# One of two copies of the transposed probabilities, taken from ScalarE to VectorE in a decoder's cross attention

## The chip, the cores and the metric

The kernel runs on one core of a Trainium2 chip. The metric is the device time of one execution in microseconds (us). For the kernel before, three executions gave 2287.59, 2289.07 and 2291.86 us; the median is 2289.07. The engines are written as in the profile: PE is TensorE (PEld its weight loads), ACT ScalarE, DVE VectorE, POOL GpSimd, and SP the engine that only starts transfers.

## What is computed

The reference is one decoder layer with three parts, each added to its input: a gated delta-rule attention, cross attention to a context, and a feed-forward part with block-quantised weights and activations. The change touches only the second:

```python
qh = q.reshape(b, s, N_GROUPS, HEADS_PER_GROUP, HEAD_DIM).transpose(0, 2, 3, 1, 4)
kh = k.reshape(b, s, N_GROUPS, HEAD_DIM).transpose(0, 2, 1, 3)
vh = v.reshape(b, s, N_GROUPS, HEAD_DIM).transpose(0, 2, 1, 3)
scores = jnp.einsum('bghsd,bgtd->bghst', qh, kh) * scale
probs = jax.nn.softmax(scores, axis=-1)
out = jnp.einsum('bghst,bgtd->bghsd', probs, vh)
...
return out @ Wc.T + bc
```

There are 8 batches of 256 tokens, 4 groups of 4 heads with 32 channels each, and 256 context rows (used as keys and as values). All is float32.

## The kernel before

Three functions follow one another. `attend` is the second: it projects the first attention's output (W_out, three matmuls for each product, since operands are split in a high and a low part), does the cross attention, and, beside that, quantises the feed-forward weights on VectorE and GpSimd. It runs from about 1560 to 2040 us of the profile. Each engine has its own instruction list, written out by hand; waits are on semaphores, and an engine works strictly in the order of its list.

**The tiles.** A batch has eight tiles (c, u): group c = 0 to 3, and u = 0 or 1 for the half of 128 tokens. I call the time between two tiles' scores a slot and name it by the tile whose scores open it. The lists run through the slots (0,0), (0,1), (1,0) to (3,1); `last_tile(b, c, u)` is the tile one slot earlier. Batches are called 0 to 7 here; batches 0 and 1 and the last two are written out, the others are a loop.

**One slot on each engine.**

- PE: `scores` of this tile (line 1531; it waits for `pt0_done` and `pt1_done` of the tile two slots before, which had the same `ps_s` banks), `turn_probs` of the last tile (line 1539, eight transposes into `ps_s[u][0]` and `ps_s[u][1]`), one to three pieces of `project` for the next batches (lines 1493 to 1495, six matmuls a piece; slots (0,1) and (1,0) have one piece each), and `mix` of the last tile (line 1549), whose first half (k = 0) waits for `pt0_done` and second half (k = 1) for `pt1_done`. In slots (3,1) and (0,0) `spread` (line 1560) comes ahead of `mix`; it waits for `rs_done`, VectorE's reciprocals. In (0,0) `keys(b, 1)` (line 1517) ends the slot, in (0,1) and (1,0) `combine(b - 1, u)` (lines 1573 to 1575).
- ACT: `turned` of the last tile (lines 1687 to 1692), the two copies from `ps_s` to `probs_t`; then `weigh` of this tile (line 1682), four exponentials that wait for VectorE's maxima. In (3,1) and (0,0) `spread` (line 1698) stands between the two.
- DVE: in some slots first `finish` (1830) and `residual` (1785), then `maxima` of this tile (line 1805, two instructions), `reciprocals` (1812) in (3,1) and (0,0), `weighted` (1819) in (0,0) and (0,1), `mixed` (1823) of the batch before in (0,1) and (1,0), then `split` (1777), layer norm (1798) and the steps of a weight chunk (1885 to 1914).
- POOL: the chunk's elementwise steps (2034 to 2050) and the powers.

`mix` for c = 0 writes `ps_v[u]` anew, so it also waits for the `mixed` of the batch before: `pe.wait_ge(mlo_done[u], b)`. For u = 0 that happens in slot (0,1), for u = 1 in (1,0). After batch 6 there are no more projections, so in batch 7, and in slots (3,0) and (3,1) of batch 6, there is nothing of `project` between `turn_probs` and `mix`.

Of the kernel before, what the change touches and what calls it, by code (L numbers as in the profile page):

```python
# [12 lines left out]
ACT = mybir.ActivationFunctionType  # L13
# [3 lines left out]
B, T, D = 8, 256, 512  # L17
# [1203 lines left out]
def attend(nc, ident, neg_half, x, ctx_in, out_t, W_out, Wc, bc, w_gate, w_up, w_down, x2_dram, xq_dram, wq_dram):  # L1221
# [10 lines left out]
    HEADS, GROUPS, HD = 16, 4, 32  # L1232
# [11 lines left out]
    with ExitStack() as st:  # L1244
        def sb(name, shape, dt):
            return st.enter_context(nc.sbuf_tensor(name, shape, dt))
# [4 lines left out]
        def two(name):  # L1251
            return [sem(f"{name}{u}") for u in U]
# [29 lines left out]
        probs_t = [sb(f"probs_t{u}", [P, 2, PER, P], F32) for u in U]  # L1282
# [24 lines left out]
        ps_s = [[st.enter_context(nc.psum_tensor(f"ps_s{u}{i}", [P, 2 * T], F32)) for i in range(2)] for u in U]  # L1307
# [17 lines left out]
        pt_ps, pt0_done, pt1_done, pv_ps = two("pt_ps"), two("pt0_done"), two("pt1_done"), two("pv_ps")  # L1325
# [12 lines left out]
        def last_tile(b, c, u):  # L1338

            return (b, c, 0) if u else (b, c - 1, 1) if c else (b - 1, GROUPS - 1, 1)  # L1340
# [3 lines left out]
        with nc.Block() as block:  # L1344
# [299 lines left out]
            def _(act):  # L1644
# [42 lines left out]
                def turned(b, c, u):  # L1687
                    act.wait_ge(pt_ps[u], GROUPS * b + c + 1)
                    act.wait_ge(pv_ps[u], GROUPS * b + c)
                    for k, done in enumerate((pt0_done, pt1_done)):  # L1690
                        act.activation(probs_t[u][:, k, :, :].rearrange("p j s -> p (j s)"), ps_s[u][k][:, :],  # L1691
                                       ACT.Copy).then_inc(done[u], 1)

                def spread(b, u):

# [70 lines left out]
                step(B - 2, True, True, False)  # L1766
                step(B - 1, True, False, False)
                turned(B - 1, GROUPS - 1, 1)
                spread(B - 1, 1)
                for u in U:  # L1770
# [3 lines left out]
            def _(dve):  # L1774
                def split(b, u, e):
                    dve.wait_ge(o_hi_done[e], 2 * b + u + 1)
                    dve.tensor_tensor(o_lo[e][:, :, :], o_raw[e][:, :, :], o_hi[e][:, :, :].bitcast(F32),
                                      ALU.subtract).then_inc(o_lo_done[e], 1)

                def residual(b, u):  # L1780

                    dve.wait_ge(y_ps[u], b + 1)
                    dve.wait_ge(x_dma[u], 16 * (b + 1))
                    dve.wait_ge(x1b_done[u], b)
                    dve.tensor_tensor(x1[u][:, :], x_in[u][:, :], ps_y[:, :], ALU.add).then_inc(x1_done[u], 1)

                def variance(b, u):
                    dve.wait_ge(x1_done[u], b + 1)
                    dve.bn_stats(stats[u][:, :], x1[u][:, :])
                    dve.drain()  # L1790
                    dve.bn_aggr(moments[u][:, :], stats[u][:, :]).then_inc(stat[u], 1)
                    dve.wait_ge(stat[u], b + 1)
                    dve.tensor_scalar(var_eps[u][:, :], moments[u][:, 1:2], LN_EPS, None, ALU.add).then_inc(var_done[u], 1)

                def layernorm(b, u):
                    dve.wait_ge(rstd_done[u], b + 1)
                    dve.wait_ge(t_ps[u], b)
                    dve.tensor_scalar(xn[u][:, :], x1[u][:, :], moments[u][:, 0:1], rstd[u][:, 0:1], ALU.subtract,
                                      ALU.mult).then_inc(xn_done[u], 1)

                def maxima(b, c, u):
                    dve.wait_ge(s_ps[u], GROUPS * b + c + 1)
                    dve.wait_ge(exp_done[u], GROUPS * b + c)
                    for i in range(2):
                        last = dve.tensor_reduce(neg_max[u][:, 2 * i:2 * i + 2],  # L1805
                                                 ps_s[u][i][:, :].rearrange("p (j t) -> p j t", j=2), AX_X, ALU.max, negate=True)
                    last.then_inc(max_done[u], 1)

                def reciprocals(b, u):
                    dve.wait_ge(exp_done[u], GROUPS * (b + 1))  # L1810
                    dve.wait_ge(spread_ps[u], b)
                    dve.reciprocal(r_sums[u][:, :], sums[u][:, :]).then_inc(rs_done[u], 1)

                def weighted(b, u):

                    dve.wait_ge(pv_ps[u], GROUPS * (b + 1))
                    dve.wait_ge(spread_done[u], b + 1)
                    mixed_heads = ps_v[u][:, :, :].rearrange("p k t -> p (k t)")
                    dve.tensor_tensor(mixed_heads, mixed_heads, r_chan[u], ALU.mult).then_inc(weighted_done[u], 1)

                def mixed(b, u):
                    dve.wait_ge(mhi_done[u], b + 1)
                    dve.tensor_tensor(mix_lo[u][:, :, :], ps_v[u][:, :, :], mix_hi[u][:, :, :].bitcast(F32),
                                      ALU.subtract).then_inc(mlo_done[u], 1)

                def finish(b, u):
                    dve.wait_ge(c_ps[u], b + 1)
                    dve.wait_ge(x1b_done[u], b + 1)
                    dve.wait_ge(x2_dma[u], 16 * b)
                    dve.tensor_tensor(x2[u][:, :], ps_t[:, :], x1b[u][:, :], ALU.add).then_inc(x2_done[u], 1)  # L1830

                def token_variance(b, u):

                    dve.wait_ge(x2_done[u], b + 1)
                    dve.bn_stats(q_stats[u][:, :], x2[u][:, :])
                    dve.drain()
                    dve.bn_aggr(q_moments[u][:, :], q_stats[u][:, :])
                    dve.drain()
                    dve.tensor_scalar(q_var[u][:, :], q_moments[u][:, 1:2], LN_EPS, None, ALU.add).then_inc(q_var_done[u], 1)
# [76 lines left out]
                def step(b, before, after, further):  # L1916
                    for c in range(GROUPS):
                        for u in U:
                            if before and (c, u) in ((1, 0), (1, 1)):
                                finish(b - 1, u)  # L1920
                            if after and (c, u) in ((1, 1), (3, 0)):
                                residual(b + 1, 1 - u)
                            maxima(b, c, u)
                            if before and (c, u) == (0, 0):
                                reciprocals(b - 1, 1)
                            if (c, u) == (GROUPS - 1, 1):
                                reciprocals(b, 0)
                            if before and c == 0:
                                weighted(b - 1, u)
                            if before and (c, u) in ((0, 1), (1, 0)):  # L1930
                                mixed(b - 1, c)
                            if after and (c, u) in ((1, 0), (1, 1)):
                                split(b + 1, 1, u)
                            if after and (c, u) == (3, 1):
                                layernorm(b + 1, 1)
                            if further and (c, u) in ((2, 1), (3, 1)):
                                split(b + 2, 0, c - 2)
                            if after and (c, u) in ((1, 1), (3, 0)):
                                variance(b + 1, 1 - u)
                            if (c, u) not in ((1, 1), (2, 1)):  # L1940
                                chunk(b, (0, 1, 2, None, 3, None, 4, 5)[2 * c + u])
                            if after and (c, u) == (2, 0):
                                layernorm(b + 1, 0)
                            if before:
                                if (c, u) == (1, 1):
                                    for tile in U:
                                        token_variance(b - 1, tile)
                                if (c, u) == (2, 0):
                                    token_norms(b - 1)
                                if (c, u) == (2, 1):  # L1950
                                    token_scales(b - 1)
                                if (c, u) == (3, 0):
                                    token_rounds(b - 1)
# [28 lines left out]
                    step(b, True, True, True)  # L1982
                step(B - 2, True, True, False)
                step(B - 1, True, False, False)
                reciprocals(B - 1, 1)
                for u in U:
                    weighted(B - 1, u)
# [479 lines left out]
```

## Time and profile before

| | us |
|---|---|
| median of three executions | 2289.07 |
| the profiled execution's own time | 2291.95 |
| span of the profiled execution, first to last instruction | 2290.2 |
| mean granted TensorE clock (share of full speed) | 0.948 |

The profile is of one execution. In the rows below, "busy" is time inside instructions, and a wait in square brackets is the idle time in front of an instruction with the one that released it. A row of several instructions (x8) shows the start of the first and the time to the end of the last. Consecutive instructions of an engine overlap a little, so the distance of two starts is what one costs in a full queue.

### The profile page before, as it was taken

Reading aid. Unit: us, or ns where it says so; the run is one execution under the profiler, and the core shown is the slowest. Engines: PE = TensorE matmul, PEld = TensorE weight load, DVE = VectorE, ACT = ScalarE, POOL = GpSimd, SP = SyncE. Lnnn points to the kernel's source line nnn. Section 1 sums busy time; section 2 is a strip of 40 time slices with the busy share of each in tenths; the row PEclk is TensorE's granted clock in tenths of the full one; section 3 lists DMA queues with packets and bytes.
Section 4 is the critical chain, followed back from the end, with each engine's and each line's share of the span. In section 5 each row is a group of like instructions: output and inputs, shape, how many; then the busy total and the mean of one; then the engine's idle time right before and its main releaser. Section 6 shows DMA issues by size and latency. Waiting matters only on the chain. (4 is left out here: it accounts for less than half of the span.)

```text
span 2290.2 us, 56662 instructions
## 1 busy us (share of the span) xinstructions
PE 2065.7 (90%) x19672; PEld 1502.0 (66%) x19672; DVE 1732.6 (76%) x4021; ACT 1530.1 (67%) x4330; POOL 709.5 (31%) x610
## 2 busy tenths in 40 slices
PE   5599899899899899899899899858999999857998
PEld 3477677677677677677677677646666666534544
DVE  7677777778777777777777777745788888755997
ACT  3588788788788788788778778735666656533343
POOL 6312112112111211211211211213576666751332
PEclk8799999999999999999999999859999999978999
DMA  3100100100100100100100100043333333222111
GB/s 76 52 10 18 38 10 12 44 10 9 47 10 9 47 10 9 47 10 9 36 21 9 33 24 9 33 143 102 99 100 101 101 101 104 67 95 81 56 53 48
DMA packets 122930, 108.19 MB, mean 47 GB/s; under 512 B 12080, under 2 KB 97072, under 8 KB 122800
## 3 DMA queue, kind: packets, MB, share of 16 engines
q1 hardware_dynamic: 122800, 106.87, 14.9%
q14 instruction: 99, 0.81, 0.1%
q8 instruction: 31, 0.51, 0.1%
HBM read 72.24 MB, written 34.60 MB: 47 GB/s over the span
## 5 line engine op out<-in xcount | busy, mean ns | idle before, releaser
L588 PE MATMUL proj<-xn_hi,w_lo 128*128 x768 | 367.5, 478 | 0.0
L589 PE MATMUL proj<-xn_lo,w_hi 128*128 x768 | 308.2, 401 | 0.0
L590 PE MATMUL proj<-xn_hi,w_hi 128*128 x768 | 306.9, 400 | 0.0
L973 DVE SCALAR_TENSOR_TENSOR qkv<-conv_in,taps,qkv 128x512 f32<-128x512 f32 x384 | 279.4, 748 | 0.0
L1194 POOL TENSOR_TENSOR o_scale<-o_var,neg_half 128x4 f32<-128x4 f32 x68 | 67.6, 1010 | 572.8 <-DVE o_var L994 572.7
L1210 POOL TENSOR_TENSOR k_len<-sumsq,pos_half 128x4 f32<-128x4 f32 x32 | 47.1, 1472 | 601.5 <-DVE sumsq L1141 601.5
L1085 DVE TENSOR_TENSOR i_less_r<-bank_c,join_mask 128x256 f16<-128x256 f32 x330 | 124.6, 418 | 104.1 <-PE bank_c L652 103.5
L892 ACT ACTIVATE inv<-bank_b 128x256 f16<-128x256 f32 x330 | 112.3, 382 | 120.2 <-PE bank_b L673 116.3
L590 PEld LDWEIGHTS proj<-xn_hi,w_hi 128*128 128x128 f32 x768 | 146.8, 191 | 35.2
L588 PEld LDWEIGHTS proj<-xn_hi,w_lo 128*128 128x128 f32 x768 | 146.4, 191 | 24.3
L1691 ACT ACTIVATE probs_t<-ps_s 128x512 f32<-128x512 f32 x128 | 69.5, 596 | 134.1 <-PE ps_s L1539 134.1
L839 ACT ACTIVATE g_mask<-mask_ge,g_cols 128x128 fp32r<-128x128 f32 x528 | 158.1, 408 | 0.0
L589 PEld LDWEIGHTS proj<-xn_lo,w_hi 128*128 128x128 f32 x768 | 148.2, 193 | 8.3
L1493 PE MATMUL ps_y<-wo_hi,o_lo 128*128 128x512 f32 x256 | 108.9, 426 | 21.8 <-DVE wo_lo L1959 18.4
L673 PEld LDWEIGHTS bank_b<-i_less_r,inv_t 64*64 64x64 f16 x2640 | 72.7, 111 | 83.3 <-issue 83.3
L673 PE MATMUL bank_b<-i_less_r,inv_t 64*64 64x64 f16 x2640 | 99.9, 198 | 27.1 <-DVE i_less_r L1085 23.5
L1805 DVE TENSOR_REDUCE neg_max<-ps_s 128x2 f32<-128x512 f32 x128 | 82.0, 682 | 54.1 <-PE ps_s L1531 53.3
L1682 ACT ACTIVATE probs<-ps_s,neg_max 128x256 f32<-128x256 f32 x256 | 117.9, 485 | 5.1 <-DVE neg_max L1805 5.1
L1114 DVE TENSOR_TENSOR v_r<-v,bank_b 128x256 fp32r<-128x256 f32 x132 | 55.6, 421 | 83.1 <-PE bank_b L700 81.4
L2308 ACT ACTIVATE g_silu<-ps_g 128x512 f32<-128x512 f32 x64 | 38.2, 597 | 118.8 <-PE ps_u L2247 118.8
L2417 POOL TENSOR_TENSOR i_q<-i,i_scale 128x1024 bf16<-128x1024 fp8e4 x32 | 61.1, 1909 | 167.5 <-DVE i L2374 167.5
L1495 PE MATMUL ps_y<-wo_hi,o_hi 128*128 128x512 f32 x256 | 102.6, 401 | 0.0
(288 smaller groups left out, 5830.4 us busy)
## 6 DMA issues: line engine op xcount, KB each, us to landing
out_t<-o_out SPq DMA_DIRECT2D x68, 256.0 KB, 2.0
o_raw<-out_t SPq DMA_DIRECT2D x32, 512.0 KB, 5.6
w_raw<-in_L_attn_W_qkv_dram SPq DMA_DIRECT2D x36, 256.0 KB, 2.9
wq_dram<-wq_q SPq DMA_DIRECT2D x48, 128.0 KB, 2.3
w_raw<-in_L_attn_W_z_dram SPq DMA_DIRECT2D x18, 256.0 KB, 2.7
x_sb<-in_x_dram SPq DMA_DIRECT2D x16, 256.0 KB, 2.8
x_in<-in_x_dram SPq DMA_DIRECT2D x16, 256.0 KB, 5.8
wq_raw<-in_L_ffn_w_gate_dram SPq DMA_DIRECT2D x16, 256.0 KB, 2.8
```

What stands on the lines that cost most here:

```text
L588: pe.matmul(out, w_lo[:, k, cols], sh.xn_hi[:, k, tok], start=(k == 0), stop=False)
L589: pe.matmul(out, w_hi[:, k, cols], sh.xn_lo[:, k, tok], start=False, stop=False)
L590: product = pe.matmul(out, w_hi[:, k, cols], sh.xn_hi[:, k, tok], start=False, stop=(k == KT - 1))
L673: last = pe.matmul(folded(bank_b[s])[rows, hb, :], inv_t[s][rows, hb, :], i_less_r[s][rows, hb, :], start=True, stop=True)
L839: last = act.activation(g_mask[s][:, i, hb, :], sh.mask_ge[:, :], ACT.Copy, scale=g_cols[:, s, 4 * i + hb:4 * i + hb + 1])
L892: act.activation(inv[s][:, :, :], folded(bank_b[s]), ACT.Copy).then_inc(t_done[s], 1)
L973: dve.scalar_tensor_tensor(out=out, in0=conv_in[:, j, :, k:k + T], scalar=taps[:, j, k:k + 1], in1=out, op0=ALU.mult, op1=ALU.add).then_in ...
L1085: dve.tensor_tensor(i_less_r[s][:, :, :], folded(bank_c[s]), bcast(sh.join_mask[:, l + 1, :], 1, 4), ALU.mult).then_inc(r_done[s], 1)
L1493: pe.matmul(ps_y[:, :], o_lo[e][:, g, :], wo_hi[:, k, :], start=begin, stop=False)
L1495: product = pe.matmul(ps_y[:, :], o_hi[e][:, g, :], wo_hi[:, k, :], start=False, stop=end)
L1682: last = act.activation(probs[u][:, j, :], ps_s[u][j // 2][:, T * (j % 2):T * (j % 2) + T], ACT.Exp, bias=neg_max[u][:, j:j + 1], accum_ou ...
L1805: last = dve.tensor_reduce(neg_max[u][:, 2 * i:2 * i + 2], ps_s[u][i][:, :].rearrange("p (j t) -> p j t", j=2), AX_X, ALU.max, negate=True)
```

## The change

ScalarE's `turned` keeps the copy for k = 0 and loses that for k = 1. VectorE gets a `turned` of its own with the copy for k = 1, with the same two waits. In every slot it stands right behind `maxima`, and so ahead of `reciprocals`, `weighted` and `mixed`; the last tile's copy stands ahead of the closing `reciprocals`. The semaphores `pt0_done` and `pt1_done` and who waits for them are as before.

```diff
@@ scalar
                 def turned(b, c, u):
                     act.wait_ge(pt_ps[u], GROUPS * b + c + 1)
                     act.wait_ge(pv_ps[u], GROUPS * b + c)
-                    for k, done in enumerate((pt0_done, pt1_done)):
-                        act.activation(probs_t[u][:, k, :, :].rearrange("p j s -> p (j s)"), ps_s[u][k][:, :],
-                                       ACT.Copy).then_inc(done[u], 1)
+                    act.activation(probs_t[u][:, 0, :, :].rearrange("p j s -> p (j s)"), ps_s[u][0][:, :],
+                                   ACT.Copy).then_inc(pt0_done[u], 1)
@@ vector
+                def turned(b, c, u):
+                    dve.wait_ge(pt_ps[u], GROUPS * b + c + 1)
+                    dve.wait_ge(pv_ps[u], GROUPS * b + c)
+                    dve.tensor_copy(probs_t[u][:, 1, :, :].rearrange("p j s -> p (j s)"),
+                                    ps_s[u][1][:, :]).then_inc(pt1_done[u], 1)
...
                             maxima(b, c, u)
+                            if before or c + u:
+                                turned(*last_tile(b, c, u))
                             if before and (c, u) == (0, 0):
                                 reciprocals(b - 1, 1)
...
                 step(B - 1, True, False, False)
+                turned(B - 1, GROUPS - 1, 1)
                 reciprocals(B - 1, 1)
```

## Rows read from the trace of the kernel before

**Rows 1.** The page's first part: busy time, share of the span, instructions

```profile
PE 2065.7 (90%) x19672; PEld 1502.0 (66%) x19672; DVE 1732.6 (76%) x4021; ACT 1530.1 (67%) x4330; POOL 709.5 (31%) x610
```

**Rows 2.** Busy time by stretch: batch 1, batch 5, and the end of batch 7

```profile
core 0: us, PE busy (x) PEld busy (x) DVE busy (x) ACT busy (x) POOL busy (x), PEclk, DMA share, GB/s
1628.30:1685.10 56.80, 53.66 (x424) 37.25 (x425) 46.69 (x97) 35.76 (x101) 40.06 (x34) 1.00 0.36 103
...
1860.00:1919.50 59.50, 56.53 (x426) 39.14 (x426) 48.23 (x99) 35.76 (x101) 40.06 (x36) 0.94 0.34 101
...
2001.60:2020.40 18.80, 13.04 (x120) 6.67 (x120) 18.24 (x44) 12.70 (x42) 16.50 (x16) 1.00 0.20 65
```

**Rows 3.** Waits of PE, batches 1 to 6: us in total, times, longest

```profile
PE ps_c L1517 <- ACT q_t L1663: 15.5, 6, 2.6
...
PE ps_s L1560 <- DVE r_sums L1812: 2.0, 1, 2.0
...
PE ps_v L1549 <- DVE mix_lo L1823: 0.4, 2, 0.3
```

**Rows 4.** Longest wait of ACT other than for the transposes, batches 1 to 6

```profile
ACT r_chan L1698 <- PE ps_s L1560: 28.6, 12, 2.7
```

**Rows 5.** Timeline of PE, batch 1, slot (0,1): start us, us, engine, line

```profile
1637.92 0.66 PE L1517 MATMUL ps_c<-ident,k_rep 128*128 128x128 f32 x4 [2.59 <-ACT q_t L1663]
...
1642.22 0.65 PE L1549 MATMUL ps_v<-probs_t,ctx_v 128*32 128x128 f32 x16 [0.18 <-DVE mix_lo L1823]
```

**Rows 6.** Timeline of DVE: batch 1, slots (0,1) and (1,0); batch 5, slot (0,1)

```profile
1640.89 0.69 DVE L1819 TENSOR_TENSOR ps_v<-ps_v,r_chan 128x512 f32<-128x512 f32 x1
1641.48 0.68 DVE L1823 TENSOR_TENSOR mix_lo<-ps_v,mix_hi 128x512 fp32r<-128x512 f32 x1
...
1648.17 0.68 DVE L1823 TENSOR_TENSOR mix_lo<-ps_v,mix_hi 128x512 fp32r<-128x512 f32 x1
...
1874.57 0.68 DVE L1823 TENSOR_TENSOR mix_lo<-ps_v,mix_hi 128x512 fp32r<-128x512 f32 x1
```

**Rows 7.** Timeline of ACT, batch 1, slot (0,1)

```profile
1641.02 1.08 ACT L1691 ACTIVATE probs_t<-ps_s 128x512 f32<-128x512 f32 x2
```

**Rows 8.** Timeline of PE, batch 1, end of slot (1,0)

```profile
1648.94 0.40 PE L1495 MATMUL ps_y<-wo_hi,o_hi 128*128 128x512 f32 x1
1649.27 0.32 PE L1549 MATMUL ps_v<-probs_t,ctx_v 128*32 128x128 f32 x4
```

**Rows 9.** Groups by line over the whole span: busy, mean ns of one, idle before

```profile
L1691 ACT ACTIVATE probs_t<-ps_s 128x512 f32<-128x512 f32 x128 | 69.5, 596 | 134.1 <-PE ps_s L1539 134.1
...
L1910 DVE TENSOR_SCALAR wq_step<-wq_step 128x512 f32<-128x512 f32 x48 | 20.4, 426 | 0.0
...
L1819 DVE TENSOR_TENSOR ps_v<-ps_v,r_chan 128x512 f32<-128x512 f32 x16 | 10.9, 681 | 0.0
```

**Rows 10.** Timeline of PE, batch 5, slot (0,1)

```profile
1872.65 1.97 PE L1539 MATMUL ps_s<-ident,probs 128*128 128x128 f32 x8
...
1876.60 0.65 PE L1549 MATMUL ps_v<-probs_t,ctx_v 128*32 128x128 f32 x16
```

**Rows 11.** Timeline of DVE: batch 2 (2,0), batch 3 (3,1), batch 4 (0,0)

```profile
1722.26 0.46 DVE L1798 TENSOR_SCALAR xn<-x,moments,rstd 128x512 f32<-128x512 f32 x1
...
1797.38 1.33 DVE L1798 TENSOR_SCALAR xn<-x,moments,rstd 128x512 f32<-128x512 f32 x1
...
1805.10 0.24 DVE L1812 RECIPROCAL r_sums<-sums 128x16 f32<-128x16 f32 x1
```

**Rows 12.** Timeline of PE, batch 4, slot (0,0)

```profile
1807.08 1.08 PE L1560 MATMUL ps_s<-ident,r_sums 128*32 128x128 f32 x32
```

**Rows 13.** Timeline of PE, batch 7: slots (0,0), (2,0) and (3,1)

```profile
1979.87 1.08 PE L1560 MATMUL ps_s<-ident,r_sums 128*32 128x128 f32 x32 [1.86 <-DVE r_sums L1812]
...
2007.39 0.92 PE L1549 MATMUL ps_v<-probs_t,ctx_v 128*32 128x128 f32 x16 [0.69 <-ACT probs_t L1691]
...
2020.48 1.08 PE L1560 MATMUL ps_s<-ident,r_sums 128*32 128x128 f32 x32 [1.51 <-DVE r_sums L1812]
```

## The prediction

> **What bounds the kernel now.** I read the busy shares first, then busy time by batch inside `attend`, then PE's waits, then the timelines of PE, DVE and ACT side by side, slot by slot. Over the whole span PE leads with 90%, DVE follows with 76%, ACT has 67% [rows 1]. The change lies in `attend` alone, so shares of the whole say little. In a full batch PE is busy 53.66 of 56.8 us, DVE 46.69, ACT 35.76 [rows 2]. So ACT, the engine that is relieved, has the most room of the three, and the one that is loaded has less.
>
> PE's list sets the pace in batches 1 to 6. It stands idle for one thing only in every batch: `keys(b, 1)` waits 2.59 us for ACT's `q_t` [rows 5], six times, 15.5 us in all [rows 3]. Before the `q_t` copy ACT does `turned`, `spread` and the exponentials, so a shorter `turned` looks useful there. It isn't: `spread` on ACT must first wait for PE's own `spread`, and that stands behind two pieces of `project` in PE's list. ACT's waits for it, in (3,1) and (0,0), are twelve with 28.6 us, 2.4 us each [rows 4]. The copy is taken from a stretch that ends in a wait.
>
> Batch 7 is another regime. With no `project` in it, PE waits for both: for ACT's copies (0.69 us ahead of `mix`) and for VectorE's reciprocals (1.86 and 1.51 us ahead of `spread`) [rows 13]. From 2001.6 to 2020.4 DVE is busy 18.24 of 18.8 us, ACT only 12.70 [rows 2]. DVE is the bound there, with half a microsecond to spare.
>
> **The price of the copy.** ACT loses 64 copies of 596 ns (half of the 128 in [rows 9]); in a full queue each frees 0.49 us (two take 1.08 [rows 7]). DVE gains 64. No float32 copy from PSUM by DVE is in the trace. The bounds are the one-input DVE instruction of the same size between SBUF tiles, 426 ns, and a two-input one that reads PSUM, 681 ns [rows 9]. I take 0.68 us, the row that shares type, size and source memory, and 0.60 us for what it adds to a full queue (the distance of the starts at 1640.89 and 1641.48 [rows 6]). The low end is 0.34 us a copy in the queue. The Trainium skill has a rule for this (VectorE: DVE Perf Modes, "Why PSUM operands drop a tier"): a PSUM operand excludes the mode that doubles a float32 copy's rate. No copy in this trace tests it; by it the upper price holds, and with the mode the low end of the sum would.
>
> **Slot (0,1), batches 1 to 6.** `mix` of tile (0,0) needs `mixed` of the batch before, which VectorE now reaches one copy later. In batch 1 `mix_lo` ends at 1641.48 + 0.68 = 1642.16, ACT's second copy at 1642.10 [rows 6, 7], and `mix` starts at 1642.22, 0.06 us behind the later, having waited [rows 5]. One copy ahead of it moves `mix` by the full 0.60. The same three rows come again in batches 2 to 4 (`mix` 0.25 us behind `mix_lo`'s end), where I take the same, so 4 x 0.60 = 2.4 us. In batches 5 and 6 PE itself ran slow here, the transposes taking 1.97 us [rows 10], so that `mix`, at 1876.60, came 1.35 us after `mix_lo` had ended [rows 6, 10]. There VectorE has also to wait for those late transposes before it can copy, and `weighted` and `mixed` queue behind; I make it 0.1 us each, 0.2 in all.
>
> **Slot (1,0), batches 1 to 6.** `mix_lo` ends at 1648.85 [rows 6], and `mix` starts at 1649.27 at its own pace, 0.33 us behind the last projection [rows 8]. Room: 0.42 - 0.06 = 0.36 us. The copy takes that up and 0.24 us more: 6 x 0.24 = 1.4 us. PE gets none of this back later, for its next wait, that for `q_t`, hangs on PE's own `spread` and moves with it. Batch 0 has no `mixed`; there only a `residual` that PE waits for can come later, between 0 and 0.6 us, of which I take 0.2, since VectorE sits in waits for GpSimd in front of it.
>
> **Other slots of batches 1 to 6: nothing.** The tightest is `spread` in (0,0). The reciprocals end at 1805.34 [rows 11] and PE takes them up at 1807.08 [rows 12]: 1.7 us of room. Ahead of them come the copies of (0,0), of (3,1) and of (3,0). The one of (3,1) fits into a stretch in which the layer norm instruction took 1.33 us where it needs 0.46 elsewhere, held by GpSimd [rows 11]. That leaves about 1.1 us. If this cover fails, 1.7 us stand against 1.7, so the cost would still be near nothing. The `mix` of these slots comes 2 us or more after the transposes, behind `project`, so an earlier second copy brings it nothing.
>
> **The seam, batch 6 slot (3,1) to batch 7 slot (0,0).** Both `spread`s wait for the reciprocals already (2.0 us [rows 3], 1.86 us [rows 13]) and VectorE never idles in between. Three copies come in, one is covered as above: 1.2 us.
>
> **Batch 7.** (0,1): 0.6 for the copy and 0.2 because it waits for slow transposes, 0.8. (1,0): here `mix` had no room, 0.6. From (1,1) to the reciprocals of (3,1), five copies are 3.0 us on a VectorE with some 0.5 us of idle time [rows 2]; ACT's 0.49 us a slot is of no use once the maxima are what the exponentials wait for. Of the rest a bit is lost in holds by GpSimd that are there anyway: 2.4 us. The closing copy ahead of the last reciprocals: 0.1.
>
> **The sum.** 2.4 + 0.2 + 1.4 + 0.2 (batch 0) + 1.2 + 0.8 + 0.6 + 2.4 + 0.1 = 9.3 us longer. The profiled execution took 2291.95 us, 0.13% above the median; against it this is 2301.2, against the median of 2289.07 it is 2298.4, which I forecast. At 0.34 us a copy, (0,1) costs 4 x 0.34, (1,0) nothing, the seam 0.7, batch 7 about 0.6 + 0.3 + 1.0: some 4 us, 2293. With no cover anywhere (0.6 in batch 0, 0.6 in (0,1) of batches 5 and 6, 1.8 at the seam, 3.0 at the end) it is 12.1, so 2301.
>
> **Rivals.** A measurement of this kernel tells some 0.2% (4.6 us) from no change.
>
> *ACT's relief decides at the end (faster).* In slots (1,1) to (3,1) of batch 7 and (3,0) of batch 6 PE waits 0.69 us for the copies [rows 13] and the exponentials begin only behind both. If VectorE's copy is cheap enough that each slot's maxima are still done when ACT's single copy is, every such slot saves 0.49 us: six make 2.9 us. It decides if a copy adds less than about 0.36 us, since then (1,0) costs nothing as well and (0,1) only about 1.4 us. Net 1.5 us less, 2287.5, and 2286 if (0,1) were hidden too. Against it stands VectorE's 97% in that stretch. To come out faster by over 0.2% more than this mechanism has would be needed; a share of chance goes there for what I can't see.
>
> *Absorbed (same).* VectorE loses up to 1 us at a time to GpSimd (1.33 against 0.46 us [rows 11]). If the copies, reading PSUM, pass while GpSimd holds the port, the later steps wait less, and the seam and the end cost under 1 us each. Then (0,1), (1,0) and a little more remain, 4 us: 2293.
>
> *TensorE's clock (slower still).* The granted clock was 1.00 in batch 1, which took 56.8 us, and 0.94 in batch 5, which took 59.5, with the same work [rows 2]; the slow stretch follows the 2.59 us wait in (0,0), and 0.94 means a few us at the lower level, 1.2 GHz. Batches 2 to 4 lie between. If the moved waits bring batch 1 into it and lengthen two others, 1.4 + 2 x 1.2 = 3.8 us come on top: 2302. The other way it could give back 2 us.
>
> *Held by GpSimd (slower still).* The layer norm instruction takes up to 0.87 us more than elsewhere when GpSimd is at work [rows 11]. Were the copy held like that, it would add that much in (0,1) and (1,0) of six batches, 10.4 us, and 2304 or later at the end. Against it: the DVE instructions that read PSUM keep to 0.68 us on average [rows 9]. The Trainium skill (SBUF — State Buffer, "Who interferes with whom") has copies in a two-port mode fight GpSimd for a port, which would be this rival if the mode held with a source in PSUM.
>
> **Chances.** The forecast with its bounds, 2294 to 2303: 0.62. Absorbed: 0.16. ACT's relief: 0.11, of which 0.06 is beyond 0.2%. Clock or port beyond 2303: 0.11. The band of 0.2% ends at 2293.6: faster 0.06, same 0.19, slower 0.75. The range leaves out the faster end and the port: 2290 to 2305.
>
> **What the changed profile would show.** A DVE COPY `probs_t` of about 0.68 us, 64 times. In (0,1) and (1,0) PE's `mix` waits for `mix_lo`, twelve times instead of two. The distance between batches' first scores grows by 0.8 us in batches 1 to 4 and less in 5 and 6. In batch 7, `spread` waits over 3 us for `r_sums`, the exponentials wait for `neg_max`, and DVE shows no idle time from (1,1) to (3,1). I am wrong if the copy takes under 0.45 us, if `mix` starts as early as before, or if the batch 7 slots get shorter.

## The result, and the profile after

The change makes the kernel slower by 0.43%: the ratio of the times is 1.0043, with a 95% interval of 1.0033 to 1.0052. The medians of 20 executions each are 2298.49 us after (2291.27 to 2304.43) and 2288.31 us before (2285.28 to 2295.39). The profiled execution after took 2301.67 us, with a span of 2299.9, so both profiled executions lie 3 to 4 us above their medians.

The page's busy shares after answer to [rows 1]:

```profile
PE 2066.6 (90%) x19672; PEld 1501.3 (65%) x19672; DVE 1764.0 (77%) x4085; ACT 1501.2 (65%) x4266; POOL 699.8 (30%) x610
```

ACT lost 29 us of work, DVE gained 31, and the time grew. The groups by line give the price of the copy, beside [rows 9]; the mean of one is in ns behind the busy us:

```profile
L1823 DVE COPY probs_t<-ps_s 128x512 f32<-128x512 f32 x64 | 43.5, 680 | 4.6 <-PE ps_s L1539 4.6
...
L1690 ACT ACTIVATE probs_t<-ps_s 128x512 f32<-128x512 f32 x64 | 38.3, 599 | 158.2 <-PE ps_s L1539 158.1
```

The 680 ns are those of the row with a PSUM operand, 681 ns. The idle time ahead of ACT's copies grew from 134.1 to 158.2 us: most of what ScalarE saved, it now waits.

Busy time after in batch 1, batch 2 and batch 5, beside [rows 2]; the granted clock stands behind POOL's busy time:

```profile
1627.70:1685.30 57.60, 53.69 (x424) 37.21 (x425) 50.13 (x106) 32.02 (x93) 37.51 (x33) 1.00 0.35 102
1685.30:1745.30 60.00, 56.73 (x426) 39.24 (x426) 52.05 (x107) 32.22 (x93) 39.17 (x35) 0.94 0.33 101
...
1863.60:1921.40 57.80, 53.68 (x424) 37.22 (x425) 51.90 (x107) 32.06 (x93) 39.18 (x35) 1.00 0.35 104
```

Batch 1 has 0.8 us more at the same clock of 1.00 and the same PE work (53.69 against 53.66 us). Batch 5 is shorter than before, at 1.00 instead of 0.94, and batch 2 longer, at 0.94 where it had 0.97.

So in batch 1 the slots can be laid side by side. PE and then DVE in the slots (0,1) and (1,0) after, beside [rows 5, 6, 8]:

```profile
1637.32 0.66 PE L1517 MATMUL ps_c<-ident,k_rep 128*128 128x128 f32 x4 [2.59 <-ACT q_t L1663]
1637.90 1.13 PE L1531 MATMUL ps_s<-k_blocks,q_t 64*128 64x512 f32 x4
...
1642.21 0.64 PE L1549 MATMUL ps_v<-probs_t,ctx_v 128*32 128x128 f32 x16 [0.78 <-DVE mix_lo L1828]
...
1645.78 1.13 PE L1531 MATMUL ps_s<-k_blocks,q_t 64*128 64x512 f32 x4
...
1649.50 0.65 PE L1549 MATMUL ps_v<-probs_t,ctx_v 128*32 128x128 f32 x16 [0.17 <-DVE mix_lo L1828]
```

```profile
1639.08 1.29 DVE L1804 TENSOR_REDUCE neg_max<-ps_s 128x2 f32<-128x512 f32 x2 [4.05 <-PE ps_s L1531]
1640.28 0.68 DVE L1823 COPY probs_t<-ps_s 128x512 f32<-128x512 f32 x1
1640.88 0.69 DVE L1818 TENSOR_TENSOR ps_v<-ps_v,r_chan 128x512 f32<-128x512 f32 x1
1641.48 0.68 DVE L1828 TENSOR_TENSOR mix_lo<-ps_v,mix_hi 128x512 fp32r<-128x512 f32 x1
...
1646.96 1.29 DVE L1804 TENSOR_REDUCE neg_max<-ps_s 128x2 f32<-128x512 f32 x2 [0.38 <-PE ps_s L1531]
1648.16 0.68 DVE L1823 COPY probs_t<-ps_s 128x512 f32<-128x512 f32 x1
1648.76 0.68 DVE L1828 TENSOR_TENSOR mix_lo<-ps_v,mix_hi 128x512 fp32r<-128x512 f32 x1
```

The copy stands between the maxima and what follows, one step of 0.60 us in the list. The wait of `mix` for `mix_lo` in (0,1) rises from 0.18 to 0.78 us, by exactly that step. In (1,0), where there was none, it is 0.17. The big wait for `q_t` is 2.59 us as before. PE's waits in batches 1 to 6, beside [rows 3]:

```profile
PE ps_c L1517 <- ACT q_t L1663: 15.6, 6, 2.6
PE ps_v L1549 <- DVE mix_lo L1828: 4.9, 11, 1.0
PE ps_s L1560 <- DVE r_sums L1811: 3.4, 1, 3.4
```

`mix` now waits eleven times where it had waited twice. The last row is the seam: `spread` in (3,1) of batch 6 waits 3.4 instead of 2.0 us.

At the end the waits of PE that have grown are those for VectorE. PE in batch 6 (3,1), then in batch 7 in (0,0), (0,1), (1,0), (2,1) and (3,1), beside [rows 13]:

```profile
1975.90 1.93 PE L1560 MATMUL ps_s<-ident,r_sums 128*32 128x128 f32 x32 [3.37 <-DVE r_sums L1811]
...
1983.39 1.08 PE L1560 MATMUL ps_s<-ident,r_sums 128*32 128x128 f32 x32 [0.94 <-DVE r_sums L1811]
...
1993.82 0.64 PE L1549 MATMUL ps_v<-probs_t,ctx_v 128*32 128x128 f32 x16 [1.98 <-DVE mix_lo L1828]
...
2002.65 0.65 PE L1549 MATMUL ps_v<-probs_t,ctx_v 128*32 128x128 f32 x16 [1.56 <-DVE mix_lo L1828]
...
2018.71 0.63 PE L1549 MATMUL ps_v<-probs_t,ctx_v 128*32 128x128 f32 x8 [1.74 <-DVE probs_t L1823]
...
2029.01 1.94 PE L1560 MATMUL ps_s<-ident,r_sums 128*32 128x128 f32 x32 [2.60 <-DVE r_sums L1811]
```

In two of the three `spread`s shown, the instructions themselves take 1.93 and 1.94 us in place of 1.08: behind the wait PE runs slow. That is no detail. The whole end, from the scores of (3,0) in batch 6 to `token_rounds` of batch 7, before and then after (granted clock behind POOL's busy time):

```profile
1964.91:2044.53 79.62, 53.29 (x496) 33.39 (x492) 60.28 (x136) 38.47 (x117) 55.41 (x50) 0.91 0.17 54
...
1966.31:2054.08 87.77, 58.17 (x496) 36.82 (x492) 65.12 (x148) 33.50 (x107) 55.95 (x52) 0.84 0.16 49
```

PE has the same 496 matmul instructions in both, and they take 4.9 us more at a granted clock of 0.84 instead of 0.91. Only the other 3.3 of the 8.15 us are added idle time of PE.

The table below serves the experiments too. "Batches 1 to 5" is the time from the first scores of batch 1 to those of batch 6. "End" is from the scores of (3,0) in batch 6 to the start of `token_rounds` of batch 7, the last part of `attend` that VectorE has. "PE busy" is the time inside PE's instructions in it, the same 496 in each kernel, and "clock" the granted clock there. Each is from one profile. e7 to e12 have `queries(b, 1)` earlier in ScalarE's list ("q early"), which is explained with e7.

| kernel | copy 2 made by | batches 1 to 5, us | end, us | PE busy in it, us | clock | ratio to before (95%) |
|---|---|---|---|---|---|---|
| before | ACT | 291.19 | 79.62 | 53.29 | 0.91 | 1 |
| changed | DVE | 293.71 | 87.77 | 58.17 | 0.84 | 1.0043 (1.0033 to 1.0052) |
| e1 | DVE at the end only | 290.24 | 87.37 | 57.76 | 0.82 | 1.0046 (1.0031 to 1.0062) |
| e2 | DVE, but for the end | 295.34 | 76.78 | 49.21 | 0.95 | 1.0015 (1.0004 to 1.0025) |
| e3 | DVE, but for (0,1), (1,0) | 292.23 | 85.94 | 58.12 | 0.83 | 1.0042 (1.0029 to 1.0055) |
| e4 | DVE, later in the slot | 290.36 | 81.66 | 53.95 | 0.88 | 1.0027 (1.0016 to 1.0038) |
| e5 | nobody | 292.20 | 76.40 | 49.80 | 0.94 | 1.0004 (0.9992 to 1.0016) |
| e6 | DVE, ACT kept busy | 293.59 | 86.20 | 55.69 | 0.87 | 1.0052 (1.0036 to 1.0068) |
| e7 | ACT, q early | 278.14 | 75.84 | 50.85 | 0.94 | 0.9925 (0.9909 to 0.9942) |
| e8 | DVE, q early | 278.45 | 83.98 | 56.16 | 0.84 | 0.9962 (0.9947 to 0.9977) |
| e9 | ACT, q early, reciprocals first | 278.17 | 77.26 | 51.43 | 0.92 | 0.9943 (0.9930 to 0.9957) |
| e10 | DVE later in the slot, else as e9 | 277.49 | 81.15 | 56.06 | 0.85 | 0.9935 (0.9922 to 0.9949) |
| e11 | as e7 | 278.14 | 75.15 | 49.24 | 0.95 | 0.9914 (0.9900 to 0.9929) |
| e12 | DVE later in the slot, q early | 277.87 | 80.48 | 53.62 | 0.87 | 0.9939 (0.9922 to 0.9956) |

With VectorE's copies in the end, the same matmuls take 53.62 to 58.17 us there, without them 49.21 to 53.29.

### The profile page after: what moved, and what is told of

Same layout as the page of the kernel before. It is cut to its first block and busy times, and to the rows that moved or that the text cites. A ratio compares the mean times of both kernels' runs of the same rounds, so it can differ in the third digit from the quotient of the medians.

```text
span 2299.9 us, 56726 instructions
## 1 busy us (share of the span) xinstructions
PE 2066.6 (90%) x19672; PEld 1501.3 (65%) x19672; DVE 1764.0 (77%) x4085; ACT 1501.2 (65%) x4266; POOL 699.8 (30%) x610
## 5 line engine op out<-in xcount | busy, mean ns | idle before, releaser
L1690 ACT ACTIVATE probs_t<-ps_s 128x512 f32<-128x512 f32 x64 | 38.3, 599 | 158.2 <-PE ps_s L1539 158.1
L1114 DVE TENSOR_TENSOR v_r<-v,bank_b 128x256 fp32r<-128x256 f32 x132 | 55.6, 421 | 83.7 <-PE bank_b L700 82.1
```

## The experiments

**Where the cost arises: e1 and e2.** Each kernel has the change in one stretch only. A predicate on the slot says who makes the second copy; both engines ask it (edits against the changed kernel, cut at the dots):

```diff
+        def on_vector(b, c, u):
+            return isinstance(b, int) and (b >= B - 1 or b == B - 2 and c == GROUPS - 1)
...
+                    for k, done in ((0, pt0_done), (1, pt1_done))[:2 if both else 1]:
+                        act.activation(probs_t[u][:, k, :, :].rearrange("p j s -> p (j s)"), ps_s[u][k][:, :],
+                                       ACT.Copy).then_inc(done[u], 1)
...
-                            if before or c + u:
+                            if (before or c + u) and on_vector(b, c, u):
                                 turned(*last_tile(b, c, u))
```

That is e1; e2 has `not (...)`. Expected of e1:

> VectorE has the second copy only from slot (3,0) of batch 6 on; before that ScalarE keeps both. My theory (VectorE is the bound there, ScalarE's relief is worth nothing): batches 0 to 5 as long as before, and 5 us more from (3,0) of batch 6 to the end of attend, so about 2293. Rival (ScalarE's copies are what PE waits for there, 0.69 us a slot): 3 us less, 2285. Rival (the loss comes from the clock or from batches 1 to 6): no change, 2288.

Expected of e2:

> The complement: VectorE has the second copy in batches 0 to 5 and in batch 6 up to (2,1), ScalarE keeps both from (3,0) of batch 6 on. My theory: about 0.8 us more in each of batches 1 to 4, some 0.3 in 5 and 6, 0.2 to 0.8 in batch 0, and the end as before: 4.5 to 5 us more, about 2293; the two halves add up to the whole change. Rival (only the end costs): 2288. Where a batch's granted clock differs its length differs by a microsecond or more on top.

e1: 2297.57 against 2288.27 us, ratio 1.0046. That is more than the 5 us expected; the sign is my theory's, the rival of a gain is out. Its batches 1 to 5 are as long as before, and its end is 87.37 us, 7.8 longer than the 79.62 of before. e2: 2292.93 us, ratio 1.0015, as expected. Its batches 1 to 5 took 295.34 us, 4.1 more. Its end runs the code of before and took 76.78, so a profile of the same code differs by 3 us there. Most of the loss is thus in the end, some 8 us or more, and 3 to 5 in the rest, where I had put about half in each. The medians of the two add up to 13.9 us, against the 10.2 of the change; the intervals are too wide to say whether the halves add up.

**Which slots of a full batch: e3.** The kernel of e1 with the predicate `(c, u) not in ((0, 1), (1, 0))` in all batches.

> VectorE has the second copy in six slots of every batch, but not in (0,1) and (1,0), where ScalarE keeps both. My theory (in batches 1 to 6 only mix_lo behind the copy in these two slots costs anything): batches 1 to 6 at the length of before at equal clock, PE's wait of mix for mix_lo back to about 0.4 us in sum; what is left is the seam and batch 7 from (1,1) on, 4 us: 2292. Rival (VectorE's added load costs PE in other slots, or the clock does): batches 1 to 4 stay 0.5 us or more longer, 2296 or later.

2299.36 us, ratio 1.0042 (1.0029 to 1.0055): not 2292. By its total alone this is the rival's 2296 or later. The mechanism holds nevertheless in the part that it was about. PE's waits in batches 1 to 6, where `mix_lo` is gone from the list:

```profile
PE ps_c L1520 <- ACT q_t L1666: 15.6, 6, 2.6
PE ps_s L1534 <- ACT r_chan L1701: 2.2, 6, 0.4
PE ps_v L1552 <- ACT probs_t L1694: 0.7, 1, 0.7
```

Batches 1 to 5 took 292.23 us, the same as in e5 (292.20), which has no DVE copy at all. So six copies a batch outside (0,1) and (1,0) cost PE nothing that can be seen beside the clock. In the end e3 pays 85.94 us, 6.3 more than before and 9.2 more than e2's, where 4 were expected. The end was mis-sized here too, and that accounts for 2 to 5 us of the 7 that were missed; where the others lie stays open.

**Load or place: e4.** VectorE's copy moves behind `reciprocals`, `weighted` and `mixed`:

```diff
                             maxima(b, c, u)
-                            if before or c + u:
-                                turned(*last_tile(b, c, u))
...
                             if before and (c, u) in ((0, 1), (1, 0)):
                                 mixed(b - 1, c)
+                            if before or c + u:
+                                turned(*last_tile(b, c, u))
```

> Same split of work, but VectorE's copy stands behind reciprocals, weighted and mixed in its slot instead of ahead of them. My theory (what costs is what queues behind the copy): the first half of mix no longer waits, the second half waits for the copy; eight matmuls of about 0.28 us cover part of it, so (0,1) costs 0.3 instead of 0.6 and (1,0) about nothing; at the seam one copy less is ahead of each spread, and one less ahead of the reciprocals of (3,1) in batch 7. Some 4.5 to 5.5 us more than before, 2293, half of the change's cost. Rival (the load counts, not the place): 2298 as with the change.

2294.53 us, ratio 1.0027 (1.0016 to 1.0038), near the 2293 expected: about 4 us of the 10 are the place, though this interval and the change's overlap a little. In batches 1 to 5 `mix` waits 1.5 us in all for `mix_lo`, where it waits 3.9 with the copy ahead. The end is 81.66 us, six shorter than with the copy ahead; 4.2 of these are PE's busy time. The first `spread` of the end shows both parts of that, a shorter wait and full speed after it:

```profile
1973.62 1.08 PE L1560 MATMUL ps_s<-ident,r_sums 128*32 128x128 f32 x32 [2.77 <-DVE r_sums L1811]
```

**What ScalarE's relief is worth: e5 and e6.** In e5 ScalarE makes the first copy, the second is left out, and PE waits for the first only (against the changed kernel; VectorE's two calls and the second wait of `scores` go too):

```diff
-                def turned(b, c, u):
-                    dve.wait_ge(pt_ps[u], GROUPS * b + c + 1)
...
-                        pe.wait_ge((pt0_done, pt1_done)[k][u], GROUPS * b + c + 1)
+                        if k == 0:
+                            pe.wait_ge(pt0_done[u], GROUPS * b + c + 1)
```

> ScalarE makes the first copy only and nobody the second; mix reads what lay in the second half of probs_t, and waits only for the first copy. Left out: the second copy of the turned probabilities, so half of the context rows are mixed with stale values. It shows what ScalarE's relief is worth alone. My theory: nothing in batches 1 to 6 (57 to 59 us each as before), since ScalarE waits for PE's spread anyway; at the end, from (3,0) of batch 6, 0.3 to 0.49 us in each of six slots and the closing one, 2 to 3 us less, 2286. Rival (ScalarE's copies hold PE in full batches too): 0.49 us or more a batch on top, 2283 or less.

2289.04 against 2288.63 us, ratio 1.0004 (0.9992 to 1.0016), where 2286 was expected. With a whole copy a slot dropped and nobody charged for it, no gain can be measured; the interval leaves room for 1.8 us. The slots of the end do get shorter in the trace, 3.60 us against 4.09 in (2,0) and (2,1) of batch 7, the 0.49 expected. That is 1 us for the two, and the next slot, (3,0), gives back 0.7 of it (4.81 us instead of 4.09). In full batches the `q_t` wait is 15.6 us, unchanged. In e6 the changed kernel gets a copy back on ScalarE that nobody needs:

```diff
                     act.activation(probs_t[u][:, 0, :, :].rearrange("p j s -> p (j s)"), ps_s[u][0][:, :],
                                    ACT.Copy).then_inc(pt0_done[u], 1)
+                    act.wait_ge(pt0_done[u], GROUPS * b + c + 1)
+                    act.activation(filler[:, :], probs_t[u][:, 0, :, :].rearrange("p j s -> p (j s)"), ACT.Copy)
```

> The change, and ScalarE gets a copy of equal size between SBUF tiles in place of the one that it lost, behind its own first copy; nobody waits for it. It shows VectorE's load without ScalarE's relief. My theory: the same as the change to 0.1%, 2298, at the most 1 us later, since the exponentials wait for VectorE's maxima or for PE's spread and not for ScalarE. Rival (ScalarE's relief had given back part of the cost): 3 us or more later than the change, 2301 to 2303.

2300.29 us, ratio 1.0052 (1.0036 to 1.0068) against the change's 1.0043 (1.0033 to 1.0052): not told apart. Batches 1 to 5 are 293.59 against 293.71 us. So e5 bounds the relief at 1.8 us. e6 agrees with none in full batches, but over the whole its interval does not rule out the 3 us of its rival.

**The wait that the change leaves alone: e7, e8, e11.** PE's 2.59 us ahead of `keys(b, 1)` are caused by ScalarE's list, in which `queries` stands behind the exponentials. ScalarE has 2.4 us of waiting for `spread` [rows 4] into which it fits:

```diff
                             if before and (c, u) == (0, 0):
+                                queries(b, 1)
                                 spread(b - 1, 1)
                             weigh(b, c, u)
-                            if before and (c, u) == (0, 0):
-                                queries(b, 1)
```

e7 is this in the kernel before, e8 in the changed one.

> The kernel before, with ScalarE's queries(b, 1) (the q_t copy of line 1663) taken from behind the exponentials of (0,0) to ahead of spread, where ScalarE waits over 2 us for PE's spread. If PE's wait of 2.59 us in keys(b, 1) is what ScalarE's list order costs, PE then waits only for the exponentials of (0,0) ahead of its transposes in (0,1), about 0.9 us later: 1.5 to 2 us less in each of seven batches and fewer slow stretches of the clock, 2273 to 2278. Rival (k_blocks or the exponentials take the wait's place): no change.

> The same move of queries(b, 1) in the changed kernel. With PE's big wait in (0,0) gone, the slots (0,1) and (1,0) start earlier against VectorE, whose copy stands ahead of mix_lo. My theory: the change costs at least as much on this base as on the old one, 10 to 14 us more than e7. Rival (the wait in (0,0) was what kept ScalarE's relief from showing): the change costs under 5 us on this base.

e7: 2270.33 against 2288.63 us, ratio 0.9925 (0.9909 to 0.9942), 18 us faster and 3 us better than the near end of what was expected. e11 is the same kernel again:

> The kernel of e7 once more, beside e12 on the same chip, to see how far a median of five or six runs repeats: 2268 to 2272. If it comes near e9's 2275.7, e9 and e7 are not told apart.

2268.75 against 2286.69 us, ratio 0.9914 (0.9900 to 0.9929). It beats both kernels of the case. PE around `keys` in e7, slots (0,0) and (0,1) of batch 1:

```profile
1633.06 0.62 PE L1549 MATMUL ps_v<-probs_t,ctx_v 128*32 128x128 f32 x16
1633.61 0.66 PE L1517 MATMUL ps_c<-ident,k_rep 128*128 128x128 f32 x4
1634.20 1.13 PE L1531 MATMUL ps_s<-k_blocks,q_t 64*128 64x512 f32 x4
1635.79 1.09 PE L1539 MATMUL ps_s<-ident,probs 128*128 128x128 f32 x8 [0.46 <-ACT probs L1682]
...
1639.22 0.82 PE L1549 MATMUL ps_v<-probs_t,ctx_v 128*32 128x128 f32 x16 [0.97 <-ACT probs_t L1691]
```

Smaller waits of 0.46 and 0.97 us take the place of the 2.59. All of batches 1 to 5 now last 55.6 us, where before they lasted 56.8 to 59.5. Busy time in two of them, with the granted clock in the column behind POOL's:

```profile
1628.30:1684.00 55.70, 53.88 (x425) 37.22 (x424) 46.44 (x97) 35.70 (x101) 39.51 (x34) 1.00 0.36 105
1684.00:1739.50 55.50, 53.68 (x425) 37.21 (x424) 48.73 (x98) 35.56 (x100) 40.55 (x34) 1.00 0.37 110
```

The clock is 1.00 in both, and the others have the same length: without the long wait there is no stretch at the lower level, 1.2 GHz. So of some 2.6 us a batch (291.19 - 278.14 = 13.05 us for five), 1.2 are waiting (56.82 of batch 1, which was at 1.00 before as well, less 55.6) and the others are the clock.

e8: 2279.80 us, ratio 0.9962 (0.9947 to 0.9977), 9.5 us behind e7, just under the 10 to 14 expected; the rival of under 5 is out. On this base the full batches of the change cost only 0.06 us each, 55.69 against 55.63. In (0,1) `mix` now waits for ScalarE's `probs_t`, so that VectorE's earlier second copy helps as much there as it hurts in (1,0). PE's waits in batches 1 to 6 of e8:

```profile
PE ps_v L1549 <- ACT probs_t L1690: 6.4, 7, 1.0
...
PE ps_v L1549 <- DVE mix_lo L1827: 1.0, 6, 0.2
```

The end is 83.98 us against 75.84 in e7 and 75.15 in e11, some 8 us, and nearly all of the difference. Most of it, 5.3 and 6.9 us, is PE's busy time.

**The end with the reciprocals first: e9 and e10.** In e9, e7's kernel with `reciprocals` ahead of `maxima`; in e10 VectorE's copy is in e4's place besides.

```diff
+                            if before and (c, u) == (0, 0):
+                                reciprocals(b - 1, 1)
+                            if (c, u) == (GROUPS - 1, 1):
+                                reciprocals(b, 0)
                             maxima(b, c, u)
```

> The kernel of e7 (both copies on ScalarE, queries(b, 1) ahead of spread), and VectorE's reciprocals taken from behind the maxima to ahead of them in (3,1) and (0,0). My theory (at the end PE's spread waits for whatever stands ahead of the reciprocals in VectorE's list): the spread waits of batch 6 (3,1), 2.0 us, and of batch 7 (3,1), 1.5 us, shrink by 1.2 us each, so some 2 us less than e7, 2268, and full batches as in e7. Rival (the reciprocals now wait for the exponentials of (3,1) and hold the maxima of (0,0) back): full batches 0.3 us or more longer, 2271 or later.

> The same with VectorE making the second copy, placed behind reciprocals, weighted and mixed. My theory: VectorE is the bound from batch 6 (3,0) on, so even the best place leaves 2 to 5 us against e9; full batches gain or lose under 0.2 us each. 2271. Rival (place was all of it): equal to e9 within 1 us, or earlier by the 0.49 us a slot that ScalarE is relieved of.

e9: 2275.72 against 2289.03 us, ratio 0.9943 (0.9930 to 0.9957), where 2268 was expected: no gain over e7, rather a loss, though the two ran on different chips. The mechanism is there, (3,1) of batch 6 took 4.82 us instead of 6.46, and full batches stay at 55.6. But (0,1) of batch 7 took 12.16 instead of 10.30 us, with this wait for `mix_lo` in it where e7 had 2.46 us:

```profile
1969.05 1.08 PE L1549 MATMUL ps_v<-probs_t,ctx_v 128*32 128x128 f32 x16 [3.61 <-DVE mix_lo L1822]
```

What was won at one VectorE wait was lost at the next: 1.15 us of the 1.86 are the longer wait. In e11, the code of e7, the same slot took 8.76 us behind the same wait of 2.46, so that the others are no more than two profiles of one kernel differ by. The median lies 5 us above e7's. The profiled execution, 2269.89 us, is the fastest of its five, and its `attend` is only 2 us longer than e7's, so where the rest of the 5 us lies stays open. e10: 2274.99 us, ratio 0.9935 (0.9922 to 0.9949), equal to e9 within the intervals. I had expected 2 to 5 us more than e9; its end has 3.9 more in the profiles (81.15 against 77.26 us), the median has nothing. So these two don't decide between load and place.

**Load or place once more: e12.** e7's list, the copy on VectorE in e4's place.

> queries(b, 1) early, reciprocals behind the maxima as in the kernel before, VectorE's copy behind reciprocals, weighted and mixed. On this base full batches have no long wait, so the place shows in them undisturbed. My theory: full batches of 55.5 us, 0.1 to 0.2 less than e7's 55.63 and e8's 55.69; from batch 6 (3,0) on some 4 us more than e7 against 8 with the copy ahead (e8). 2274. Rival (the load counts): 2279 as e8.

2275.38 against 2286.69 us, ratio 0.9939 (0.9922 to 0.9956), beside e11's 2268.75 on the same chip. Full batches are 55.47 to 55.77 us, level with e7. The end is 80.48 us, against 75.15 with both copies on ScalarE and 83.98 with the copy ahead. Both theories have their share: in this place VectorE's load still costs 5 us at the end, and the place ahead adds some 3.5. Of the 5 us, 4.4 are PE's busy time and 1.0 its idle time (53.62 against 49.24, 26.86 against 25.91), so the load costs more by the pace of PE than by its waits. Between e12 and e8 the ratios alone decide nothing (0.9939 against 0.9962, with intervals that overlap); the 3.5 us are those of the two profiles.

## Why the prediction was right, and where it was not

The sum was right: 9.3 us against 2289.07 predicted, 10.2 measured between the medians. Its parts were not all of the right size, and that the total fits so well is in part luck: batches 1 to 5 paid 1.2 us less than forecast and the end 3 us more. The parts in the profiles sum to more than the whole, since what lies ahead of the first scores, which the change leaves alone, was 2.0 us shorter in the one after. Batch 0, forecast at 0.2 us more, took 56.66 instead of 55.28 us; without VectorE's copy it took 53.69 to 56.59 in other profiles, so that this term is not measured. The upper bound was added up wrong by a little: the terms named there make 11.9 us, not 12.1.

**The price.** 0.68 us a copy and 0.60 in the list were predicted; 680 ns and 0.60 measured. The trace agrees with the Trainium skill's rule on PSUM operands (VectorE: DVE Perf Modes, "Why PSUM operands drop a tier"): 680 ns, where the one-input instruction between SBUF tiles takes 426 [rows 9]. No copy is longer than 0.69 us, so the rival of a hold by GpSimd is out.

**Slots (0,1) and (1,0).** In batch 1, at equal clock, (0,1) grew from 7.29 to 7.88 us and (1,0) from 7.04 to 7.28: 0.59 and 0.24 against 0.60 and 0.24. In (1,0) it is the same in all of batches 1 to 6, 7.03 to 7.05 us before and 7.28 or 7.29 after. The whole of batches 1 to 5 grew by 2.5 us, against 3.7 predicted; e2 and e6 have 4.1 and 2.4. The clock lies over it, as the five batches differ by up to 2.7 us within one profile. Taken apart, the forecast is met: PE's idle time in these batches grew from 15.40 to 18.95 us, by 3.55, as its waits for `mix_lo` did (0.4 to 3.9), and its busy time shrank from 275.78 to 274.76. In e3, without these two copies, the time for the other six is not to be seen.

**ScalarE's relief is worth nothing.** Right in full batches and, as far as a measurement can tell, in the end: at most 1.8 us by e5. Three slots show small gains, (3,0) of batch 6 with 4.06 instead of 4.27 us, (1,1) of batch 7 with 3.47 instead of 3.68 and (2,0) with 4.01 instead of 4.09. From (2,1) on they are gone: 5.57 instead of 4.09, with VectorE's copy as what `mix` waits for.

**The end, the step that was too small.** The seam was to cost 1.2 us, (0,1) and (1,0) of batch 7 1.4, and (1,1) to the end 2.5: 5.1 us. The profiles say 2.1, 2.2 and 3.8, together 8.15. All of the 5.1 were waits; the waits measured, PE's added idle time, are 3.3, and what I had at nothing, the pace of the same matmuls, is 4.9. So the step that failed is the one that left the clock out at the end. It shows in single places: the `spread` of (3,1) in batches 6 and 7 took 1.93 and 1.94 us instead of 1.08 behind the longer waits, 1.7 us in sum, and (0,1) of batch 7, forecast at 0.8 us, grew by 1.6, with scores of 2.08 us instead of 1.52 ahead of the wait. A slow PE behind a wait I had put only among the rivals, and only for full batches. The first of the two ran slow behind its wait of 3.37 us in the change, e1, e3 and e8, and took 1.08 us behind waits of 2.24 in e5 and 2.77 in e4. The length of the wait alone doesn't decide it, though: in e12 it took 1.94 us behind one of 2.77, and behind one of 1.97 it took 1.56 in e7 and 1.08 in e11, which is the same code. What else decides it stays open. Besides, I let holds by GpSimd absorb more than they did. The one that I worked out was right: the layer norm behind the copy took 0.87 us instead of 1.48 in (3,1) of batch 6, so it absorbs 0.61. But the copy in (3,1) stands ahead of the reciprocals and the absorbed time behind them, which helps only the next slot. From the scores of (1,1) to the start of the last `spread` but one PE took 22.79 instead of 20.01 us, 2.8 more, where I had 2.4 and five copies are 3.0.

**The clock rival.** It was meant as an addition, and so it is one at the end, with more than half of what the end pays. In full batches it moved single batches both ways: batch 2 at 59.9 us after and 58.2 before, batch 5 at 57.9 after and 59.5 before. It did not sum to a cost.

**The signs.** Of those named, the copy's 0.68 us, the waits for `mix_lo` (eleven of the twelve) and three of the first four batches' 0.8 us came (0.82, 1.77, 0.76 and 0.83). In batch 7 no `spread` waited over 3 us: that wait, 3.37, stands in batch 6, and batch 7 has 0.94 and 2.60. The exponentials waited for `neg_max` once, 1.6 us, and VectorE kept 2.6 us of waits from (1,1) to (3,1), where it had 2.3 before.

## What to carry to other kernels

Before work goes to another engine, follow what is queued behind the place where it lands. Here the relieved engine ended its slots in waits, the loaded one had the low parts that TensorE waited for, and 0.60 us of list order came through as 0.59 us of time. Look apart at the last iterations of a pipelined loop, where the work that covered everything has run out. Compare TensorE's busy time for the same instructions too, and not only its waits: at the end here it was the larger part of the loss. And a wait of TensorE that recurs in every iteration can cost more than its length: here 1.2 us less waiting a batch saved 2.6; to fill it, move something from behind it into a wait of the engine that it waits for.

## What was not expected of the hardware

Moving one 0.6 us copy in ScalarE's list gained 18 us (ratios 0.9925 and 0.9914), while PE's waits of 2.59 us add up to only 18 us over seven batches and waits of 1.4 us came in their place. The remainder is TensorE's clock: with the 2.59 us wait in each batch, its matmuls after it ran slow in most batches (transposes at 1.97 us [rows 10]), and with none over 1 us in batches 1 to 5 the granted clock stayed 1.00 and every batch took 55.6 us. The clock also makes a good part of this kernel's noise: the same code took 79.62 and 76.78 us for the end in the profiles of before and e2, with PE busy for 53.29 and 49.21 us at granted clocks of 0.91 and 0.95. And it makes work for another engine dear: in three pairs of profiles (changed and before, e8 and e11, e12 and e11) VectorE's copies added 1.0 to 3.3 us of idle time to PE's end, and 4.4 to 6.9 us to the time of its matmuls. Each figure is of one profile, and the two of one code above lie 4.1 us apart, but no kernel without these copies in the end is as slow there as the fastest with them (53.29 against 53.62 us).
